# V of a local attention projected once per token, and the product with V by key blocks in 32-row tiles

## The reference, cut to what matters

```python
def attn_layer(x, Wqkv, qs, ksc, Wo):                 # x: 16 sequences, 256, 128
    q, k, v = heads(x @ Wqkv)                         # 16 heads of 64
    q, k = l2norm(q) * qs, l2norm(k) * ksc
    q, k = rope(q, scale), rope(k, 1 / scale)
    bk2, bv2 = look(blocks_of_32(k)), look(blocks_of_32(v))   # each block with the one before it: 64 keys
    sim = einsum('bhwie,bhwje->bhwij', blocks_of_32(q), bk2) * 8
    mask = (it < jb) | (it > jb + 32) | (jb == -1)
    attn = softmax(where(mask, -big, sim), -1)
    return einsum('bhwij,bhwje->bhwie', attn, bv2).reshape(...) @ Wo
def ffn_layer(x, ...):
    a, gate = split(layernorm(x) @ W1 + b1)           # 341 and 341
    return a * gelu(gate) @ W2 + b2
```

## Time and profile before

| | us |
|---|---|
| median of 3 runs | 6836.91 (6830.29 to 6841.93) |
| the profiled execution | 6825.92, of which span 6824.1 |
| mean granted TensorE clock in it | 0.886 |
| PE, DVE, ACT, POOL busy | 5375.1, 3781.1, 3227.5, 2650.2 |

### The profile page before, as it was taken

One profiled execution on the slowest core, in us unless ns is written; L12 is line 12 of the kernel. 1 busy time (PEld: TensorE's weight loads), 2 busy tenths in 40 slices (PEclk: granted clock), 3 DMA queues, 4 the chain that ended last, 5 costly groups with the idle time before them and its releaser, 6 DMA issues. The chain is left out here.

```text
span 6824.1 us, 165871 instructions
## 1 busy us (share of the span) xinstructions
PE 5375.1 (79%) x70742; PEld 3275.5 (48%) x70742; DVE 3781.1 (55%) x5248; ACT 3227.5 (47%) x4705; POOL 2650.2 (39%) x1366
## 2 busy tenths in 40 slices
PE   4649999999999999999999997699997444444446
PEld 3326565666566556656655664345444221222234
DVE  3256666766666666666666664433332544444554
ACT  1225655555555555555555554233333334333235
POOL 0025555555555555555555553111111444444500
PEclk9669999999999999999999998788887777777778
DMA  0010001000000100010000000000000000000000
GB/s 20 0 38 16 15 16 34 15 17 26 21 17 16 28 20 15 15 34 16 16 26 21 16 17 12 6 2 2 2 2 5 3 2 2 2 2 1 0 14 17
DMA packets 168350, 93.76 MB, mean 14 GB/s; under 512 B 122170, under 2 KB 155843, under 8 KB 167747
## 3 DMA queue, kind: packets, MB, share of 16 engines
q1 hardware_dynamic: 167747, 84.17, 4.4%
HBM read 23.75 MB, written 3.67 MB: 4 GB/s over the span
## 5 line engine op out<-in xcount | busy, mean ns | idle before, releaser
L926 POOL TENSOR_TENSOR tf_qk<-tf_qk,tf_rot 128x1024 f32<-128x1024 f32 x384 | 907.4, 2363 | 1613.6 <-DVE tf_rot L1284 1613.6
L1861 PE MATMUL mb_psum<-mb_read,ident 128*128 128x512 f32 x512 | 376.5, 883 | 604.3 <-POOL mb_read L1795 604.3
L979 PE MATMUL tf_psum<-tf_Wqkv,tf_xsT 128*128 128x512 f32 x1536 | 753.2, 613 | 72.7 <-issue 30.6
L933 POOL TENSOR_TENSOR tf_qk<-tf_qk,tf_rn 128x1024 f32<-128x1024 f32 x384 | 722.9, 1903 | 162.3 <-ACT tf_rn L1168 162.3
L996 PE MATMUL tf_psum<-tf_Wqkv,tf_xsT 128*64 128x512 f32 x3072 | 743.8, 605 | 7.0 <-ACT tf_V L1172 1.9
L1161 ACT ACTIVATE tf_sq<-tf_psum 128x1024 f32<-128x1024 f32 x384 | 393.5, 1025 | 594.6 <-DVE tf_rot L1284 594.6
L1280 DVE TENSOR_TENSOR tf_qk<-tf_psum,tf_table 128x1024 f32<-128x1024 f32 x384 | 470.2, 1224 | 332.1 <-PE tf_psum L979 329.7
L1795 POOL TENSOR_TENSOR mb_read<-mb_state,mb_Csb 128x512 f32<-128x512 f32 x256 | 396.0, 1575 | 657.4 <-DVE mb_state L2012 644.5
L1290 DVE TENSOR_REDUCE tf_ss<-tf_sq 128x16 f32<-128x1024 f32 x384 | 466.3, 1214 | 261.7 <-ACT tf_sq L1161 261.7
L1861 PEld LDWEIGHTS mb_psum<-mb_read,ident 128*128 128x128 f32 x512 | 130.4, 278 | 755.7 <-POOL mb_read L1795 636.8
L1172 ACT ACTIVATE tf_V<-tf_psum 128x1024 f32<-128x1024 f32 x384 | 395.6, 1030 | 175.4 <-PE tf_psum L996 169.9
(11 more groups left out here) (295 smaller groups left out, 9563.1 us busy)
## 6 DMA issues: line engine op xcount, KB each, us to landing
tf_zr<-z SPq DMA_DIRECT2D x96, 128.0 KB, 2.7
z<-tf_z SPq DMA_DIRECT2D x48, 256.0 KB, 2.4
tf_Wqkv<-in_Wqkv_split SPq DMA_DIRECT2D x18, 512.0 KB, 3.8
tf_zu<-z SPq DMA_DIRECT2D x97, 64.0 KB
tf_zu<-z SPq DMA_DIRECT2D x97, 63.5 KB
tf_zsh<-tf_z SPq DMA_DIRECT2D x96, 64.0 KB
tf_zsh<-tf_z SPq DMA_DIRECT2D x96, 63.5 KB
tf_Wo<-in_L_ffn_Wo SPq DMA_DIRECT2D x6, 512.0 KB, 4.3
```

The lines of the kernel that those rows point to most:

```text
L926: nc.gpsimd.tensor_tensor(v, v, rot[:, kind, :], ALU.add).then_inc(added.sem, 1)
L933: nc.gpsimd.tensor_tensor(v, v, rn[:, t, HEADS * kind:HEADS * (kind + 1)].unsqueeze(2) .to_broadcast([P, HEADS, HD]), ALU.mult).then_inc(n ...
L979: last = nc.tensor.matmul(proj[:, half, :], xsT[:, step.unit(0), WIN + t * P:WIN + (t + 1) * P], Wqkv[:, c:c + 512], start=True, stop=True)
L1861: last = nc.tensor.matmul(y_ps[:, :], k.ident[:, :], read[:, m % 2, j, :, :], start=(m == 0 and j == 0), stop=(m == STEPS - 1 and j == 1), ...
```

## The change

V of every token is projected once. A tile's four blocks of 32 tokens are split by parity: for an even block the result goes to 32 partitions (0 or 64, by the parity of the head), for an odd block to the next 32. `project_v` is one part of eight products with 32 output rows each; all four column tiles of `score` are in use. `V` keeps four tiles (`v_slot`), since the last block of a tile is needed by the next one.

The 64 keys of a window then lie on partitions by the parity of their block, not by before and own. For even windows the score product reads its keys with the two blocks swapped, and the mask is swapped in the same rows.

`attend` is in two halves. `attend(step, 0)` multiplies the even key blocks (32 rows, 64 output rows) with the queries of both windows that see them, 64 columns; `attend(step, 1)` the odd blocks: block 1 with 64 columns, block 3 with the 32 of its own window, and on a second tile block 3 of the tile before with 32. All add up in PSUM on two one-column products with a zero matrix (`zerob`). The second half waits for the end of the first.

The orders change. PE: project q, (xn), scores, transposes of the probabilities, output, project k, transposes of q, `attend 0`, transposes of k, `attend 1`, (`widen` or `narrow`), (input), `project_v`, (`widen 2`). ACT: (xn's copy), square of q, copy of the probabilities, exponential, copy of q, square of k, copy of k, `keep_out`, `inverse_norm`, (GELU), (input's copy), `keep_v`, (GELU 2). The fills of `trans` follow as x, p, q, k, input. At the head of a unit the projection of q waits for the input's copy.

```diff
@@ Step
+    def v_slot(self, lag):
+        return (self.k - lag) % 4
...
-        V = sb("V", [P, TT, WPT, PAIRS, HD])
+        V = sb("V", [P, 4, WPT // 2, PAIRS, HD])
...
@@ def project
+                    if kind == 0 and not (isinstance(step.I, int) and tau == 0):
+                        pe.wait_ge(copied, place(step.before(), "input") + 2)
...
-            def project_v(step, part):
+            def project_v(step):
                 tau, t = step.tile(2), step.t(2)
-                if part == 0:
-                    if t == 0:
-                        pe.wait_ge(v_ok.sem, v_ok.at(step.I * 4 + (step.k // 2 - 1), 1))
-                    pe.wait_ge(centred.sem, centred.at(tau, 1))
-                else:
-                    pe.wait_ge(v_kept.sem, v_kept.at(tau, 1))
-                for j in range(2):
-                    w = t * WPT + 2 * part + j
+                if t == 0:
+                    pe.wait_ge(v_ok.sem, v_ok.at(step.I * 4 + (step.k // 2 - 1), 1))
+                pe.wait_ge(centred.sem, centred.at(tau, 1))
+                for m in range(2):
                     for odd in range(2):
-                        c = 2 * INNER + odd * 512
-                        last = nc.tensor.matmul(score[64 * odd:64 * odd + 64, j, :],
-                                                xsT[:, step.unit(2), w * WIN:w * WIN + 2 * WIN], Wqkv[:, c:c + 512],
-                                                start=True, stop=True)
+                        for parity in range(2):
+                            x = WIN + t * P + (2 * m + parity) * WIN
+                            r, c = 64 * odd + 32 * parity, 2 * INNER + odd * 512
+                            last = nc.tensor.matmul(score[r:r + 32, m, :], xsT[:, step.unit(2), x:x + WIN], Wqkv[:, c:c + 512],
+                                                    start=True, stop=True)
                 last.then_inc(v_done.sem, 1)
...
@@ def scores
-                pe.wait_ge(v_kept.sem, v_kept.at(tau - 1, 2))
+                pe.wait_ge(v_kept.sem, v_kept.at(tau - 1, 1))
...
+                            keys = kT[r, pair, at:at + 2 * WIN].rearrange("p (b j) -> p b j", b=2)
+                            if w % 2 == 0:
+                                keys = keys[:, ::-1, :]
...
-            def attend(step):
+            def attend(step, parity):
                 tau, t = step.tile(3), step.t(3)
-                pe.wait_ge(copied, place(step, "p") + 2)
-                pe.wait_ge(v_kept.sem, v_kept.at(tau, 2))
-                pe.wait_ge(z_added.sem, z_added.at(tau - 1, 1))
-                nc.tensor.matmul(mixed[:, 0, 0:1], identb[:, :], identb[:, 0:1], start=True, stop=True)
+                if parity == 0:
+                    pe.wait_ge(copied, place(step, "p") + 2)
+                    pe.wait_ge(v_kept.sem, v_kept.at(tau, 1))
+                    pe.wait_ge(z_added.sem, z_added.at(tau - 1, 1))
+                    for odd in range(2):
+                        nc.tensor.matmul(mixed[:, odd, 0:1], zerob[:, :], identb[:, 0:1],
+                                         start=True, stop=False, skip_group_check=True)
+                    windows = [(0, 0), (2, 0)]
+                else:
+                    pe.wait_ge(pv_done.sem, pv_done.at(tau, 1))
+                    windows = [(1, 0), (3, 0)] + ([(3, 1)] if t else [])
                 for j in range(PAIRS // 2):
-                    for w in range(WPT):
+                    for v, back in windows:
+                        lo, hi = (0, WIN) if back else (v * WIN, min(v + 2, WPT) * WIN)
                         for half in range(2):
                             for odd in range(2):
-                                r, c, pair = slice(64 * odd, 64 * odd + 64), slice(64 * half, 64 * half + 64), j + 4 * half
-                                last = nc.tensor.matmul(mixed[c, odd, j * P + w * WIN:j * P + (w + 1) * WIN],
-                                                        V[r, t, w, pair, :], probT[r, t, pair, w * WIN:(w + 1) * WIN],
-                                                        start=True, stop=True)
+                                r = slice(64 * odd + 32 * parity, 64 * odd + 32 * parity + 32)
+                                pair = j + 4 * half
+                                last = nc.tensor.matmul(mixed[64 * half:64 * half + 64, odd, j * P + lo:j * P + hi],
+                                                        V[r, step.v_slot(3 + back), v // 2, pair, :],
+                                                        probT[r, t, pair, lo:hi],
+                                                        start=False, stop=True, skip_group_check=True)
                 last.then_inc(pv_done.sem, 1)
...
-            def keep_v(step, part):
-                act.wait_ge(v_done.sem, v_done.at(step.tile(2), part + 1))
-                nc.scalar.activation(V[:, step.t(2), 2 * part:2 * part + 2, :, :].rearrange("p w a e -> p (w a e)"),
-                                     flat2(score), ACT.Copy).then_inc(v_kept.sem, 1)
+            def keep_v(step):
+                act.wait_ge(v_done.sem, v_done.at(step.tile(2), 1))
+                nc.scalar.activation(V[:, step.v_slot(2), :, :, :].rearrange("p m a e -> p (m a e)"), flat2(score), ACT.Copy)\
+                    .then_inc(v_kept.sem, 1)
...
@@ def keep_out
-                act.wait_ge(pv_done.sem, pv_done.at(step.tile(3), 1))
+                act.wait_ge(pv_done.sem, pv_done.at(step.tile(3), 2))
...
@@ shape_constants
+    even = (np.arange(P) // WIN % 2 == 0)[:, None, None]
+    local = np.where(even, np.roll(local, WIN, axis=2), local)
```

More of the change, by code:

```diff
@@ L638, in fills @@
         if self.has(1):
-            names.append("q")
+            names += ["q", "k"]
         if self.has_input():
             names.append("input")
-        if self.has(1):
-            names.append("k")
         return names
@@ L706, in transformer_stage @@
         identb = sb("identb", [P, P], BF16)
+        zerob = sb("zerob", [P, P], BF16)
         zu = sb("zu", [P, TT, P])
@@ L1109, in body @@
                     project(step, 0)
+                if ff == 1:
+                    turn_xn(step)
                 if step.has(2):
                     scores(step)
-                if ff == 1:
-                    turn_xn(step)
                 if step.has(3):
@@ L1122, in body @@
                 if step.has(3):
-                    attend(step)
-                if step.has_input():
-                    turn_input(place(step, "input"), step.I * 4 + (step.k // 2 + 1))
-                if step.has(2):
-                    project_v(step, 0)
+                    attend(step, 0)
                 if step.has(1):
                     turn_part(step, 1)
+                if step.has(3):
+                    attend(step, 1)
                 if ff == 1:
@@ L1135, in body @@
                     narrow(step)
+                if step.has_input():
+                    turn_input(place(step, "input"), step.I * 4 + (step.k // 2 + 1))
                 if step.has(2):
-                    project_v(step, 1)
+                    project_v(step)
                 if ff == 2:
@@ L1141, in _ @@
             pe.wait_ge(zeroed, 5)
-            pe.wait_ge(masks_ready, 3)
+            pe.wait_ge(masks_ready, 4)
             turn_input(0, 0)
@@ L1221, in body @@
                     inverse_deviation(step.pair())
+                elif ff == 1:
+                    copy_xn(step)
                 if step.has(0):
                     square(step, 0)
-                if ff == 1:
-                    copy_xn(step)
                 if step.has(3):
@@ L1231, in body @@
                     copy_part(step, 0)
-                if step.has_input():
-                    copy_input(place(step, "input"), (step.k // 2 + 1) % 4)
+                if step.has(0):
+                    square(step, 1)
+                if step.has(1):
+                    copy_part(step, 1)
                 if step.has(3):
                     keep_out(step)
-                if step.has(0):
-                    square(step, 1)
-                if step.has(2):
-                    keep_v(step, 0)
-                if step.has(1):
-                    copy_part(step, 1)
                 if step.has(0):
@@ L1247, in body @@
                     gelu(step.pair(), 1)
+                if step.has_input():
+                    copy_input(place(step, "input"), (step.k // 2 + 1) % 4)
                 if step.has(2):
-                    keep_v(step, 1)
+                    keep_v(step)
                 if ff == 2:
@@ L1265, in _ @@
             nc.vector.memset(eps[:, :], LN_EPS).then_inc(masks_ready, 1)
+            nc.vector.memset(zerob[:, :], 0.0).then_inc(masks_ready, 1)
             dve.wait_ge(mults, 16 * DEPTH)
```

11 lines of the change are left out of this document (5 added, 6 removed).

## The result

The changed kernel takes 7058.55 us, the median of 4 runs (7047.94 to 7093.32); the kernel before, run beside it, 6833.6 (6814.03 to 6841.93). The ratio is 1.0342, with a 95% interval of 1.03 to 1.0384: 3.4% slower, where 3.0% faster was forecast, above the range of 6580 to 6760 us.

What follows compares the result with a forecast made beforehand. PE's in-order queue was taken as the bound, busy 73.0 of 75.86 us in four steps. Terms summed to 71.54, -4.32, by 48 a gain of 207 us: median 6630 us, 3.0% less, range 6580 to 6760.

Steps and rivals of the forecast that it cites:

- Moved at no cost: Input's transposes moved behind the feed-forward: V's 1.87 us cover the copy, POOL and SP queues keep their order, no cost.
- s+8.3: ScalarE's copy of the input, about 8.3 us after s, the start of q's transposes; PE needs it at s+9.7.
- the late xn: PE's transposes of xn, now ahead of the scores, reach xn before VectorE ends it: a stall of 0.26 us.
- `widen 2`: Its 0.91 us wait for a gate and 0.07 of drained pipeline go in every fourth step: -0.98 us.
- the stall of `keep_out`: PE waits behind attend 1 for ScalarE to copy out the PSUM banks: 1.45 us (widen 0, narrow) or 1.21 (widen 1).
- rival 1: V's four column tiles run only two at a time, block 3.74 us: 6977 us, slower; chance 0.08.
- rival 2: In small tiles loads lie beside the streams, 27 ns for each of 24 rounds: 6706 us, smaller gain; chance 0.16.
- rival 3: Tiles of 32 rows that add up in PSUM take rounds twice as long: 7011 us, slower; chance 0.06.
- rival 4: PE's issue gaps, 2.5 us in eight steps, vanish or double as its program moves in memory: 48 us either way.
- The copy of q: PE's transposes of k, behind attend 0, wait for ScalarE's copy of q: a stall of 0.07 us per step.
- the gain from xn's place: Transposes of xn go ahead of the scores, so mask and scores cover their copy: -2.05 us every fourth step.
- the step of kind 0: The step in four whose feed-forward adds nothing: 16.09 us becomes 14.73.

Runs made afterwards that it cites:

- e1: Changed kernel with SP's signals that weights are in place moved ahead of the loads of the next unit's input: 6843.27 us, ratio 1.0007.
- e3: Changed kernel with the input's transposes and their copy back in mid-step, SP's queue as in the changed kernel: 6904.29 us, ratio 1.0093.
- e10: e8 with SP's signals behind the loads of the input again: 6789.04 us, ratio 0.9923 to the kernel before.
- e5: e1 with five never-read products of 512 columns put into PE's wait for keep_out: 6755.69 us, ratio 0.9874 to the kernel before.
- e6: e1 without VectorE's clamp of the sums of squares, a small addend in ScalarE's logarithm instead: 6911.29 us, ratio 1.0108 to the kernel before.
- e4: Kernel before, with only the transposes of xn and their copy moved ahead of the scores: 6744.11 us, ratio 0.9862.
- e8: e7 without the clamp and with three more reorderings, of attend 0, keep_out, xn and the square of k: 6460.47 us, ratio 0.9444 to the kernel before.
- e9: Kernel before, V still in two parts, with SP's signals ahead of the input's loads and xn's transposes ahead of the scores: 6721.79 us, ratio 0.9825.
- e7: e1 with V's projection and the input's transposes ahead of widen 0 and narrow, copies likewise: 6536.4 us, ratio 0.9557 to the kernel before.

## Why the prediction was wrong

**The step that failed** is "Moved at no cost", and in it the sentence "The POOL and SP queues keep their order". The order is kept, and that is the trouble: `turn_input` moved to the end of the step, SP's loads wait for it, and SP's signal for the next unit stands behind the loads. The prediction followed the moved transposes to their copy on ScalarE and not to the DMA issues that wait for the buffer they read. (The copy starts at s+9.41, 1768.93 on ScalarE's timeline, where s+8.3 was forecast, and the projection hardly notices: in e1 PE waits for it 21 times, 5.1 us in all.) e1, e3 and e10 show it from three sides. Two such waits in four steps are 5.5 us. With the late xn, +1.08, and `widen 2`, which kept 0.67 of the 0.98 that was to go, they are 7.25 of the 7.57 us that the four steps shown miss.

In the whole: the stage took 219 us more in place of 207 less, a miss of 426. The four steps, at the 2.4 GHz level throughout, give 7.57x48 = 363. The other 63 are put down to the clock and to waits for SP that are longer elsewhere (3.07 us in the mean for 2.71). How these two share is open: a spell costs nothing while PE waits, so half of the added 235 us at 1.2 GHz, 118, is only its upper bound.

**The clock** has no term in the prediction. It priced the stall of `keep_out` by its length, and the length was right (1.37 and 1.23 for 1.45 and 1.21). e5 shows that in e1 the idle time brings on spells worth 88 us more. In the changed kernel itself more of the spells begin at the wait for SP (47) than at `keep_out` (29).

**xn** was forecast 0.26 late and was 1.34 in the step shown. The forecast moved DVE's chain ahead by square 1's earlier place and kept the clamp at nothing. The chain did move (its sum of squares starts at s+3.98, forecast s+4.06), and that is what brings the clamp to the start of POOL's multiplication of the probabilities, to whose end it is held. Before it came 1.2 us or more into that operation. DVE's and POOL's timelines of the changed kernel in that step:

```profile
1746.91 1.16 DVE L1305 TENSOR_REDUCE tf_ss<-tf_sq 128x16 f32<-128x1024 f32 x1
1748.10 1.82 DVE L1312 TENSOR_SCALAR tf_ss<-tf_ss 128x32 f32<-128x32 f32 x1
1749.84 2.69 DVE L1357 TENSOR_SCALAR tf_xn<-tf_zsh,tf_moments,tf_rstd 128x128 f32<-128x128 f32 x4
```
```profile
1747.97 1.92 POOL L944 TENSOR_TENSOR tf_prob<-tf_prob,tf_rden 128x1024 f32<-128x1024 f32 x1
1750.52 3.79 POOL L936 TENSOR_TENSOR tf_qk<-tf_qk,tf_rn 128x1024 f32<-128x1024 f32 x2 [0.64 <-ACT tf_rn L1184]
```

The clamp ends at 1749.92, POOL's operation at 1749.89, and 190 of the 192 clamps start under this operation and end with it. The Trainium skill ("SBUF — State Buffer", "SBUF: two separate sides") says that VectorE and GpSimd share one pair of ports as an exclusive lock: GpSimd's operations take it, and of VectorE's those in a 2-port mode or with two SBUF inputs, each for a whole instruction, while the other blocks. The trace agrees: an operation of 0.18 us takes 1.82. That the clamp runs in such a mode no trace shows.

**`widen 2`** was to lose its whole wait (0.91) and kept 0.6, on PE's timeline of the changed kernel in kind 2:

```profile
1790.56 1.95 PE L1104 MATMUL tf_psum<-tf_xnT,tf_W 128*85 128x512 f32 x4 [0.61 <-DVE tf_hT L1365]
```

The held clamp also delays the chain behind it: in e6, without the clamp, PE's waits of this kind fall from 43 to 3.

**What was right.** V's 128x32 tiles run four at once (16 records in 1.86 us from start to start, 1747.63 to 1749.49 in the step of kind 0), so rival 1 falls. A round of 64 columns costs 1.16/16 = 0.073 us with the block's edges, and eight rounds more of 32 columns 1.60-1.13 = 0.47, 0.059 each. `attend 0` (64 columns throughout) takes 0.03 more than `attend 1` on a first tile (half its rounds 32 columns): 4 ns a round, where rival 2, loads beside the streams, needs 27. (The prediction's "leave 27 for a load" is a slip: 62.5 less 27 is 35. The 27 more for a round of 64 columns don't hang on it.) The Trainium skill ("TensorE: Matmul & The Clock Gate", part 3) lets a load overlap running products only when its row group is another. That rule, by which rival 2 would hold, isn't borne out by these tiles; the same part also names loads into a background weight buffer, which would fit them. Rounds of 0.06 to 0.07 are also the end of rival 3, and rival 4's 48 us is not the size of the miss. The copy of q, the wait for `keep_out`, the gain from xn's place (e4, 97 us for 98) and the step of kind 0 came out as worked. What the change sheds on PE is real, and e8 (6460) shows a kernel with it that beats the best one without it that was tried (e9, 6721.79). Both rivals that were slower priced products, and no rival priced a queue.

**Left open:** why some idle time brings the clock down and other idle time, as that at xn's copy, rarely did; what the idle time without a shown releaser is, at the head of each round of e1; and V once without any change of order, which was not tried.

## What to carry to other kernels

When a step is moved, follow its buffer to the queue that refills it, and read that queue's program to the next signal: what stands behind the refill is late by the whole move. Put signals that are ready ahead of waits for other things. A forecast stall on TensorE is best filled with work that is already due (V and the input in e7, part of its 307 us), since its price is more than its length where the granted clock falls after it; and a small VectorE operation belongs into a pause of POOL.

## What the runs showed of the hardware

- **VectorE held by GpSimd.** A 128x32 tensor_scalar takes 0.18 us alone and 1.8 us when it starts at the beginning of POOL's 1.9 us multiplication (190 of 192 in the changed kernel); four 128x128 ones take 1.10, 2.69 or 5.95 us by what POOL does at the time. The operations with PSUM inputs and the reductions kept their 1.2 us beside the same POOL work.
- **The clock after short idle time.** In e1, 87 of 102 spells at 1.2 GHz begin at PE's 140 waits of 1.2 to 1.4 us; in e10, all 68 at its 95 waits for SP of 3.0 us in the mean. The stage before had 14. Five products of 512 columns in the wait of e1 left 18.
- **A DMA issue on SP that takes 2.7 us.** Of the three issues of an input's load two take 0.7 us (0.69, 0.76) and the third, of one row, 2.72, and whatever stands behind it on SP's queue waits.
- **Four column tiles of 32 with 512 columns** run at once in float32: 16 records in 1.86 us, as long as 8 records on tiles of 64 columns of the array before (1.87).
